# Gram products of a gated delta rule in four column tiles, with the order of the last stores and scalings changed

## The reference, cut to what matters

```
q = l2norm(silu(conv(x @ Wq))) * SCALE; k = l2norm(silu(conv(x @ Wk))); v = silu(conv(x @ Wv))
for t in range(512):
    S = S * exp(g[t])
    delta = (v[t] - k[t] @ S) * beta[t]
    S = S + outer(k[t], delta)
    o[t] = q[t] @ S
```

## Time and profile before

| | before |
|---|---|
| median of 3 runs | 2737.78 us (2733.69 to 2740.29) |
| profiled execution, its own time | 2728.86 us |
| its span | 2727.1 us |
| TensorE busy | 2487.7 us, 91% |
| VectorE busy | 1859.3 us, 68% |
| GpSimd busy | 1355.5 us, 50% |
| ScalarE busy | 1269.0 us, 47% |
| mean granted clock of TensorE | 0.955 |

### The profile page before, as it was taken

How to read it: one execution, slowest core, us unless ns; L and a number is a source line. 1 busy time by engine, 2 the same in 40 slices (tenths; PEclk the granted TensorE clock), 3 DMA queues, 4 the chain that set the end, 5 groups by cost and what they waited for, 6 DMA issues and landing times.

```text
span 2727.1 us, 33296 instructions
## 1 busy us (share of the span) xinstructions
PE 2487.7 (91%) x11786; PEld 1462.5 (54%) x11786; DVE 1859.3 (68%) x2240; ACT 1269.0 (47%) x2029; POOL 1355.5 (50%) x609
## 2 busy tenths in 40 slices
PE   7999949999999999999588899999989888999998
PEld 2554624444677999865133333333433333777776
DVE  5668875554655666676689889889988897722223
ACT  4434225531223666443557655765665442334333
POOL 0222338860050000250599999999999994222221
PEclk9989769989899999999799899999999999999999
DMA  6444874332063777641364674666567555000000
GB/s 229 143 124 105 96 117 97 89 101 93 12 232 134 266 271 269 205 133 41 112 197 160 178 225 164 205 193 194 180 202 213 185 206 210 1 1 16 16 0 31
DMA packets 246199, 384.98 MB, mean 141 GB/s; under 512 B 127104, under 2 KB 148608, under 8 KB 238624
## 3 DMA queue, kind: packets, MB, share of 16 engines
q1 hardware_dynamic: 232912, 335.45, 39.3%
q0 software_dynamic: 9296, 38.80, 5.7%
q10 hardware_dynamic: 3840, 8.72, 0.9%
HBM read 312.91 MB, written 59.51 MB: 137 GB/s over the span
## 4 chain that ended last, share of the span: by engine, by line
PE 58%; DVE 11%; POOL 9%; issue 8%; DMA 5%; SPq 4%; ACT 3%; POOLq 0%; ACTq 0%; DVEq 0%; PEldq 0%
PE psum L2058 7%; POOL arena L813 5%; PE psum L2005 4%; PE psum L2239 4%; PE psum L2240 4%; PE psum L2871 4%; POOL arena L805 3%; SPq L2317 3%; DMA arena<-bc_scr 3%; PE psum L3060 2%; PE psum L2212 2%; PE psum L2213 2%; PE psum L1901 2%; PE psum L485 2%; PE psum L1903 2%
## 5 line engine op out<-in xcount | busy, mean ns | idle before, releaser
L805 POOL TENSOR_TENSOR arena<-arena 128x2048 f32<-128x2048 f32 x128 | 600.8, 4694 | 110.0 <-DVE arena L1570 76.6
L2058 PE MATMUL psum<-arena,cst 128*128 128x512 f32 x1024 | 496.7, 620 | 93.9 <-POOL arena L813 84.1
L1106 ACT ACTIVATE psum<-arena,negA 128x512 f32<-128x512 f32 x512 | 333.6, 682 | 281.2 <-DVE arena L1585 240.5
L2058 PEld LDWEIGHTS psum<-arena,cst 128*128 128x128 f32 x1024 | 187.0, 193 | 385.8 <-issue 206.5
L1585 DVE TENSOR_TENSOR_SCAN arena<-psum,arena 128x512 f32<-128x512 f32 x256 | 310.8, 1214 | 99.5 <-POOL arena L805 57.8
L813 POOL TENSOR_TENSOR arena<-arena 128x1024 f32<-128x1024 f32 x128 | 324.0, 2531 | 18.2 <-DVE arena L1585 9.1
L1585 DVE TENSOR_TENSOR_SCAN psum<-psum,arena 128x512 f32<-128x512 f32 x256 | 296.8, 1204 | 0.0
L857 POOL TENSOR_TENSOR arena<-arena 128x512 f32<-128x512 f32 x64 | 92.4, 1443 | 325.5 <-ACT arena L1230 300.5
L2005 PE MATMUL psum<-arena 128*128 128x512 f32 x512 | 230.7, 594 | 1.3 <-PE psum L2005 0.8
L2403 POOL TENSOR_TENSOR arena<-arena,cst 128x512 f32<-128x512 f32 x64 | 76.2, 1218 | 257.4 <-DVE arena L2723 165.3
L2239 PE MATMUL psum<-r 128*128 128x512 f32 x512 | 202.8, 396 | 1.0 <-issue 1.0
(11 more groups left out here) (374 smaller groups left out, 5017.4 us busy)
## 6 DMA issues: line engine op xcount, KB each, us to landing
arena<-bc_scr SPq DMA_DIRECT2D x256, 512.0 KB, 4.8
arena<-w_exp SPq DMA_DIRECT2D x23, 1408.0 KB, 6.3
arena<-in_gu SPq DMA_DIRECT2D x48, 512.0 KB, 5.1
arena<-in_inw SPq DMA_DIRECT2D x32, 512.0 KB, 3.7
arena<-in_dn SPq DMA_DIRECT2D x31, 512.0 KB, 6.9
x_scr<-arena SPq DMA_DIRECT2D x19, 512.0 KB, 5.9
arena<-in_x SPq DMA_DIRECT2D x8, 1024.0 KB, 9.6
w_exp<-in_gu SPq DMA_DIRECT2D x16, 512.0 KB, 6.8
```

What stands on the lines that cost most here:

```text
L805: nc.gpsimd.tensor_tensor(dB[:, at:at + 2], du[:, j:j + 2].unsqueeze(1).broadcast_to([P, 2, 2, T]), BR[:, q % 2].unsqueeze(2).broadcast_to ...
L1106: nc.scalar.activation(psum[:, bank], dt[:, b % 2, j + t], ACT.Exp, scale=negA2[:, at:at + 1]).then_inc(s["da_ok"], 1)
L2058: ins = mm(psum[:, t], ident, dB[:, k % NSLOT, t], start=False, stop=(n == NS - 1), skip_group_check=True)
```

## The change

The Gram products swap their operands. The chunk's keys and queries, kept side by side in `KQC`, are now the weights, 128x32, and the block diagonal slot is moved through, 128 columns. Four chunks go to four column tiles, one PSUM bank takes a group of 16. The result is turned, so ScalarE copies it to SBUF (`gram_copy`) and TensorE transposes it in four pieces (`gram_turn`) into the bank that VectorE masks from. In passes 1 to 3 there is one bank for products and one for the transposed group; after the last pass two and two. Further:

- ScalarE writes the keys beside the queries (`keys_beside`) once a batch.
- `gram_evict` 0, 1 and 2 move behind `conv_tile` 3, 5 and 7.
- In pass 3 SP stores the Gram rows of batch 2 before it waits for the inverse of batch 1; the eight stores of that inverse go to ScalarE's queue.
- After the last pass ScalarE spreads the four slots of group 2 (eight instructions), GpSimd the rest; eviction 3 of batch 3 comes after row 12 of the inverse of batch 2 instead of after row 14; both halves of V are scaled after the last inverse.
- On SP's queue, the eight large loads of V for the second head group all come behind the stores of the inverse of batch 2, where four of them stood before, and four small ones of the first head group move behind the last Gram rows.

```diff
...
-KQ = view(0, 8192, "p (s l t) -> p s l t", s=2, l=TL)
+KQ = view(0, 4096, "p (s l t) -> p s l t", s=1, l=TL)
+KQC = view(4096, 4096, "p (u g c m) -> p u g c m", u=2, g=HG, c=NCH)
 QT = view(8192, 4096, "p (l t) -> p l t", l=TL)
...
     if b == B - 1:
-        at = qks[:, n % 4]
+        at = vst[:, n % 4] if n // 4 % 4 == 2 else qks[:, n % 4]
     else:
...
+def gram_tmp(b, k):
+    return MT[:, 4 * (k % 2)] if b == B - 1 else MT[:, 0] if b == B - 2 else LTB[:, B - 1]
+def gram_banks(b, k):
+    return (k % 2, 2 + k % 2) if b == B - 1 else (0, 1)
 def key_rows(b, i):
-    return acc[:, i] if b == B - 1 else KQ[:, 1, i * B + B - 1]
+    return acc[:, i] if b == B - 1 else MT[:, 4 * i + 1] if b == B - 2 else (LT, LTB)[i][:, TL - 1]
 dec = sb("dec", [P, 4, TL * NCH])
...
                 values(0, h, 0, B - 1, "v_in")
-        if b >= 2:
+        if b == B - 2:
             inverse_out(b - 2)
...
             gram_out(b - 1)
+        if b == B - 1:
+            sp.wait_ge(s["pt_ok"], b - 1)
+        if b:
             gram_in(b - 1)
...
+    keys_out(B - 1)
     sp.wait_ge(s["vt_out"], 16 * B)
-    for h in range(8):
-        values(0, h, B - 1, B, "v_in")
     for h in range(4):
-        values(1, h, 0, B, "v_in1")
-    keys_out(B - 1)
+        values(0, h, B - 1, B, "v_in")
     sp.wait_ge(s["g_out"], 16 * B)
...
     gram_in(B - 1)
-    inverse_out(B - 2)
     for h in range(4, 8):
+        values(0, h, B - 1, B, "v_in")
+    inverse_out(B - 2)
+    for h in range(8):
         values(1, h, 0, B, "v_in1")
...
         l, t = k // 8 * B + b, 64 * (k % 8)
+        if n >= 16 * (B - 1) + 8 and n < 16 * (B - 1) + 12:
+            continue
         if k == 0:
...
         if n >= 4:
-            pool.wait_ge(s["g1_mm"], n - 3)
+            pool.wait_ge(s["g1_mm"], n - 7 if n >= 16 * (B - 1) + 12 else n - 3)
         nc.gpsimd.tensor_tensor(gram_slot(b, n).rearrange("p c (h j) -> p c h j", h=8),
...
             act.wait_ge(s["k_out"], 32 * b)
+        if b == B - 2:
+            act.wait_ge(s["m_out"], 32)
         nc.scalar.copy(key_rows(b, i), psum[:, ring_bank("k", b, i)]).then_inc(s["kc_ok"], 1)
+    def gram_copy(b, k):
+        n = 4 * b + k
+        act.wait_ge(s["g1_mm"], 4 * n + 4)
+        act.wait_ge(s["g1_t"], n - 1 if b == B - 1 and k > 1 else 4 * b if b == B - 1 else n)
+        if b >= B - 2:
+            act.wait_ge(s["m_out"], 16)
+        nc.scalar.copy(gram_tmp(b, k), psum[:, gram_banks(b, k)[0]]).then_inc(s["gc_ok"], 1)
+    def keys_beside(b):
+        act.wait_ge(s["bc_used"], 4 + 4 * (b + 1))
+        nc.scalar.copy(KQC[:, b % 2, :, :, 0:CH],
+                       KQ[:, 0, b::B].rearrange("p g (c i) -> p g c i", i=CH)).then_inc(s["gc_ok"], 1)
     for b in range(B):
...
                                      scale=convw[:, c, 3:4]).then_inc(s["first_ok"], 1)
+                if b and c == 0:
+                    keys_beside(b - 1)
                 if b and c in (1, 3):
...
                                      ACT.Sqrt, bias=epsc[0:64, 0:1]).then_inc(s["std_ok"], 1)
+            if b and c in (1, 3, 5, 7):
+                gram_copy(b - 1, c // 2)
         for i in range(4):
...
         for i in range(4):
+            if b == B - 1 and i == 2:
+                act.wait_ge(s["pt_ok"], b - 1)
+                for h in range(8):
+                    act.dma_start(t_scr[b - 2, 16 * h:16 * h + 16].rearrange("j (l q r) -> q (j l) r", l=HG, q=16),
+                                  PT[b - 2][16 * h:16 * h + 16].rearrange("p j (l u) i -> p (j l) (u i)", u=2)
+                                  ).then_inc(s["t_out"], 16)
             act.wait_ge(s["g_mm"], 8 * b + 4 + i + 1)
...
     act.wait_ge(s["conv_ok"], 2 + NQKV * B)
+    keys_beside(B - 1)
     keys_copy(B - 1, 0)
     keys_copy(B - 1, 1)
+    l, t = 1 * B + B - 1, 0
+    for h in range(8):
+        ins = nc.scalar.activation(vst.rearrange("p j (c m) -> p (j c) m", c=4)[:, :, CH * h:CH * h + CH],
+                                   KQ[:, 0, l, 0:256].rearrange("p (c j) -> p c j", j=CH),
+                                   ACT.Identity, scale=bmask[:, h:h + 1])
+    ins.then_inc(s["ka_ok"], 1)
+    for k in (0, 1, 2, 3):
+        gram_copy(B - 1, k)
...
         n, l, at = 4 * b + k, k // 2 * B + b, slice(256 * (k % 2), 256 * (k % 2) + 256)
-        dve.wait_ge(s["g1_mm"], 4 * n + 4)
-        g = psum[:, n % 2].rearrange("p (c w i) -> p c w i", w=2, i=CH)
+        dve.wait_ge(s["g1_t"], n + 1)
+        g = psum[:, gram_banks(b, k)[1]].rearrange("p (c w i) -> p c w i", w=2, i=CH)
         v.tensor_tensor(MT[:, l, at].rearrange(c3, i=CH), g[:, :, 0], LTB[:, l, at].rearrange(c3, i=CH), ALU.mult)
...
                 dve.wait_ge(s["zr_out"], 16 * NZERO)
+            if b == 3 and hg == 1:
+                dve.wait_ge(s["k_out"], 64)
             dve.wait_ge(s["ab_mm"], 2 * b + hg + 1)
...
         decay_columns(0)
-        evict(0)
         conv_tile(3)
+        evict(0)
         invert(8, 10)
         conv_tile(4)
-        evict(1)
         invert(10, 11)
...
         conv_tile(5)
+        evict(1)
         invert(11, 12)
...
         conv_tile(6)
-        evict(2)
         invert(12, 13)
         conv_tile(7)
+        evict(2)
         dve.wait_ge(s["std_ok"], b + 1)
...
         invert(13, 16)
-        if b == B - 1:
-            dve.wait_ge(s["k_out"], 32 * b)
         for i in range(4):
             dve.wait_ge(s["bc_mm"], 4 * b + i + 1)
-            dst = KQ[:, 1 - i // 2, (i % 2) * B + b]
-            v.scalar_tensor_tensor(out=dst, in0=qks[:, i], scalar=SCALE if i < 2 else 1.0,
-                                   in1=psum[:, 3 - i % 2], op0=ALU.mult, op1=ALU.mult).then_inc(s["bc_used"], 1)
+            if i < 2:
+                v.scalar_tensor_tensor(out=KQC[:, b % 2, i, :, CH:2 * CH], in0=qks[:, i].rearrange(c3, i=CH), scalar=SCALE,
+                                       in1=psum[:, 3 - i % 2].rearrange(c3, i=CH), op0=ALU.mult, op1=ALU.mult).then_inc(s["bc_used"], 1)
+            else:
+                v.scalar_tensor_tensor(out=KQ[:, 0, (i % 2) * B + b], in0=qks[:, i], scalar=1.0,
+                                       in1=psum[:, 3 - i % 2], op0=ALU.mult, op1=ALU.mult).then_inc(s["bc_used"], 1)
         dve.wait_ge(s["bc_used"], 4 + 4 * (b + 1))
         for hg in range(HG):
-            ch.link(v.tensor_tensor(QT[:, hg * B + b], KQ[:, 1, hg * B + b], tmpA[:, 2 + hg], ALU.mult))
+            ch.link(v.tensor_tensor(QT[:, hg * B + b].rearrange(c3, i=CH), KQC[:, b % 2, hg, :, CH:2 * CH],
+                                    tmpA[:, 2 + hg].rearrange(c3, i=CH), ALU.mult))
     dve.wait_ge(s["ab_used"], 2 + 2 * B)
...
     inverse_first(B - 2)
-    for k, (i0, i1) in enumerate(((1, 8), (8, 10), (10, 13), (13, 15))):
+    for k, (i0, i1) in enumerate(((1, 8), (8, 10), (10, 12), (12, 13))):
         inverse_rows(B - 2, i0, i1)
         gram_evict(B - 1, k)
-    inverse_rows(B - 2, 15, 16)
-    dve.wait_ge(s["v_in"], 256)
-    ch.link(v.tensor_tensor(V[:, 0:B], V[:, 0:B], bcol[:, 0:B].unsqueeze(3).broadcast_to([P, B, NCH, DV]), ALU.mult))
+    inverse_rows(B - 2, 13, 16)
     inverse_first(B - 1)
     inverse_rows(B - 1, 1, CH)
+    dve.wait_ge(s["v_in"], 256)
+    ch.link(v.tensor_tensor(V[:, 0:B], V[:, 0:B], bcol[:, 0:B].unsqueeze(3).broadcast_to([P, B, NCH, DV]), ALU.mult))
     dve.wait_ge(s["v_in1"], 128)
...
-        n, l = 4 * b + k, k // 2 * B + b
-        if n >= 2:
-            pe.wait_ge(s["g_ev"], n - 1)
+        n = 4 * b + k
+        to = psum[:, gram_banks(b, k)[0]]
+        pe.wait_ge(s["gc_ok"], 5 * b + 1 + k - (b == B - 1 and k > 0))
         for j in range(4):
-            pe.wait_ge(s["kx_ok"], 4 * n + j + 1)
+            if b == B - 1 and k == 2:
+                pe.wait_ge(s["ka_ok"], 1)
+            else:
+                pe.wait_ge(s["kx_ok"], 4 * n + j + 1 - 4 * (b == B - 1 and k == 3))
             for c in range(4):
-                at, t = 32 * (4 * j + c), 256 * (k % 2) + CH * (4 * j + c)
-                ins = mm(psum[:, n % 2, at:at + 32], gram_slot(b, j)[:, c], KQ[:, :, l, t:t + CH], start=True, stop=True)
+                ins = mm(to[32 * c:32 * c + 32, colq[j]], KQC[:, b % 2, k // 2, 16 * (k % 2) + 4 * j + c], gram_slot(b, 4 * n + j)[:, c], start=True, stop=True)
             ins.then_inc(s["g1_mm"], 1)
+    def gram_turn(b, k):
+        n = 4 * b + k
+        pe.wait_ge(s["gc_ok"], 5 * b + 2 + k)
+        if n:
+            pe.wait_ge(s["g_ev"], n - (b == B - 1 and k > 0))
+        for t in colq:
+            ins = nc.tensor.transpose(psum[:, gram_banks(b, k)[1], t], gram_tmp(b, k)[:, t], ident)
+        ins.then_inc(s["g1_t"], 1)
     for b in range(B):
...
                 gram_group(b - 1, c // 2)
+            if b and c in (2, 4, 6):
+                gram_turn(b - 1, c // 2 - 1)
         for i in range(4):
             gate_tile(i)
+            if b and i == 0:
+                gram_turn(b - 1, 3)
         pe.wait_ge(s["rinv_ok"], b + 1)
...
     keys_t(B - 1, 1)
-    for k in range(4):
-        gram_group(B - 1, k)
```

(9 more changed lines are left out.)

20 lines of the change are left out of this document (10 added, 10 removed).

## The result

| | before | after |
|---|---|---|
| median (range, runs) | 2739.61 us (2733.69 to 2748.72, 5) | 2762.47 us (2755.95 to 2765.45, 5) |
| ratio, 95% interval | | 1.0074 (1.0054 to 1.0093) |
| profiled execution, its span | 2728.86, 2727.1 us | 2758.65, 2756.9 us |
| mean granted clock | 0.955 | 0.954 |
| TensorE, VectorE busy | 2487.7, 1859.3 us | 2451.3, 1867.5 us |

The change made the kernel 22.9 us slower in the medians. The forecast was 11.1 us: the direction was right, the size half, and 2762.47 lies above the forecast range of 2731 to 2755. TensorE has 36 us less to do and the program is longer, as in the forecast.

The account below looks back on a forecast made before the run. TensorE narrowly bounds pass 1, VectorE passes 2 and 3; behind them VectorE, DMA and SP's queue take turns. 5.4 + 1.0 + 0.3 + 4.4 = +11.1 us on the median 2737.78 gave 2748.9, range 2731 to 2755.

Parts of the forecast that it names:

- pass 1: Projection stage, batch 1: TensorE's waits for later evictions, with half clock behind them, delay the norms; +5.4 us.
- pass 2: Projection stage, batch 2: VectorE sets it and reaches the norms almost together with TensorE; +1.0 us.
- the end: Behind the stage: Gram rows leave 9.6 us sooner, SP's queue adds 2.0 + 12.0 before the inverse's stores; +4.4 us.
- VectorE's own durations: Projection stage: VectorE's scans, convolutions and evictions take the times read from the earlier trace, such as 11.75 us to eviction 0.
- Half clock: TensorE behind each new wait of the stage: runs at half clock for a while, adding 1.8 us.
- the wait for G: Behind the stage: VectorE's 5.56 us wait for batch 2's masked Gram rows shrinks to about 0.9, gain 4.7.
- Price of a group: Gram products on TensorE: four column tiles cut a group from 3.6 to 1.0 us, saving 26 us in twelve groups.
- The PSUM rule: Gram groups of the stage: tiling speeds the products, not the emptying of PSUM, which can become the limit; no size.
- (A): Rival, projection stage: the waits cost no half clock; +5.8 us, 2743.6; chance 0.15.
- (B): Rival, SP's queue: V issues at their mean cost; +6.7 us, 2744.5, chance 0.15; with (A) 2739, chance 0.07.
- (C): Rival, SP's queue: it keeps up and VectorE's inverse ends the stage, -9.6 there; 2735 or 2729.6; chance 0.16.
- (D): Rival, Gram groups: column tiles do not overlap, a group stays 3.5 us plus 0.4; 2760 and more; chance 0.05.

Follow-up runs that it names:

- experiment 2: The change with matmuls computing nothing wanted put into TensorE's two large waits of each pass; 2755.47 us, one run.
- experiment 1: The change with TensorE's transpositions of groups 1, 2 and 3 moved later, nothing else; median 2742.44 us, ratio 0.9988 to the kernel before.
- experiment 7: The change with transpositions of groups 1 to 3 later and four large V loads back ahead of the last Gram rows; 2722.00 us, ratio 0.9945.
- experiment 8: experiment 7 plus nine matmuls computing nothing wanted before the second norms of passes 2 and 3; median 2721.44 us, ratio 0.9928.
- experiment 5: The kernel before with only four large V loads moved behind the stores of the inverse of batch 2; 2746.47 us, one run.
- experiment 3: The change with VectorE's evictions 0 to 2 back at their places before it; 2756.45 us, one run.
- experiment 9: The kernel before with only the change's order behind the stage, Gram products and V loads untouched; median 2734.27 us, ratio 0.9985.
- experiment 4: The change with SP's eight V loads of pass 3 moved behind the store and loads of batch 2's Gram rows; 2764.52 us, one run.

## Why the forecast was right in direction and half in size

Of the 11.4 us that are missing in the forecast 2.9 lie in pass 1, 3.6 in pass 2, 2.1 in pass 3 and 2.8 in the end. Three steps failed. VectorE's own durations were taken as fixed, where they grow inside GpSimd's slots: the largest miss, in pass 2. Half clock was put at 1.8 us a wait, where it cost 2.3 to 2.4. And the wait for G was put at 0.9 us, where two waits of 5.5 stood. The chain of waits in which these terms stand was right. The upper end of the range, 2755, is also 3 us more than its own terms give (2737.8 + 10 + 4.4 = 2752).

**Price of a group, right.** 1.01 us for 1.0. TensorE's saving was real and, as forecast, not counted where it then waits.

**Pass 1, right in place, 2.9 us short.** Taken from the start of the pass (0.85 us later than before), VectorE's scans start at 97.6 (97.5 forecast); eviction 0 ends at 112.6 for 111.5, of which 0.9 is L2712 beside GpSimd's slots; scans 1 start at 120.2, 7.6 us later for 7.0, which is half clock at 2.4 for 1.8; eviction 1 ends 9.9 us behind that for 9.2, the scans L2704 at 2.12 where the row behind the earlier trace rows had 1.46; the norms start 23.6 behind it for 23.1, half clock again. So one term was mis-sized, half clock (1.8 from three waits of 2.6 us; waits of 5 to 6 cost 2.3 to 2.4, and experiment 2 measures 2.25), and one was missing, VectorE beside GpSimd. I had taken VectorE's durations from where they stood and not asked at what other time the slots would be spread once the groups moved; the earlier trace rows had 6.26 us between its scans and convolution 5, and the same work takes 4.7 in experiment 1 (116.39 to 121.07).

**Pass 2, VectorE last as forecast, +4.6 for +1.0.** VectorE's own list took 3.45 us more. In the forecast's terms: from the first scans to the end of eviction 0 it allowed 14.0 us and the trace has 16.0 (183.81 to 199.78), from the second scans to the norms 33.7 and the trace has 34.4 (206.86 to 241.28), and the first scans start 0.55 later than forecast, behind the slow row of 144. The step that failed is that VectorE's durations in the earlier trace rows would stay. That VectorE and TensorE would come to the norms almost together held: VectorE waits 0.64 us. Part of the difference is scatter: the list of the kernel before gave 81.60, 83.83 and 84.43 us in three kernels, that of the change 86.20, 86.12 and 86.12. Traces show what scatters: a wait of TensorE before the second norms. In experiments 1 and 7, which run the same list there, TensorE's timeline reads, in experiment 1:

```profile
225.85 3.78 PE L2970 MATMUL psum<-arena,cst 32*128 32x512 f32 x4 [1.77 <-DVE arena L2769]
229.56 4.94 PE L2944 MATMUL psum<-arena,wab 128*48 128x512 f32 x8
```

and in experiment 7:

```profile
225.03 1.98 PE L2972 MATMUL psum<-arena,cst 32*128 32x512 f32 x4 [0.37 <-DVE arena L2771]
226.94 3.63 PE L2946 MATMUL psum<-arena,wab 128*48 128x512 f32 x8
```

A wait of 1.77 us with half clock behind it, 3.78 + 4.94 us, against one of 0.37 and full clock, 1.98 + 3.63; both sets start 75.1 us into the pass, so the 3.1 us between the two passes (84.60 and 81.54) are half clock alone, and experiment 8, with this wait filled, has 81.64. In experiment 7 TensorE had been slow earlier, a projection of 6.59 us behind a wait of 3.99, where VectorE was last anyway, and came to the norms without a wait. Where the clock falls decides it. Against the mean of the three (83.3) the change costs pass 2 2.9 us; pass 3, 79.8 in the mean, 1.8. The forecast of 1.0 and 0.3 stays too small, since it left VectorE's slowing out. In pass 3 VectorE is busy for 68.55 us where it was for 66.97, and it waits 1.54 us for the second decay product (292.02), where it had waited 0.85 for the first.

**The end, +7.2 for +4.4.** Term by term: eviction 3 sooner by 4.9, right. G sooner by 4.7: not there, and the step that failed is the wait of "about 0.9", what the eight issues leave behind the norm products. It left out that SP's store stands behind projection 7 (the V loads wait for it) and 15 us of V issues, and that the stage's own waits push projection 7 back; experiment 1, where they don't, has 4.4 of it. From eviction 3 to the stores 43.6 us for 30.3, +13.3, where 2.0 + 12.0 were forecast, right (experiment 5 has 11.8 for the four large ones). From the stores to the chain 9.8 for 11.0, where no change was forecast: -1.2.

**The rules.** The PSUM rule cited in the forecast holds: with the products at 1.0 us TensorE waited 32.1 us in eight waits of the stage for evictions (L2659), and in experiment 3, where they came sooner, 22.0 for the copies out of PSUM. But it was their order and not their amount: in experiment 1 the same evictions, from later places of the transpositions, cost 6.1 us in three waits. A rule that bears on the missing term was not used: the Trainium skill (SBUF — State Buffer, Who interferes with whom) has VectorE and GpSimd share a pair of SBUF ports, and a VectorE instruction with two inputs in SBUF contend there with a GpSimd instruction that reads SBUF, while one with at most one such input, outside the modes of two ports, does not. The rows agree: L2712 and L2704, with both operands in SBUF, lose 0.9 us inside a slot, about the 1.05 us that one slot instruction takes alone (GpSimd's at 327.54 in experiment 9), and the convolutions, with one in PSUM, lose nothing. The small copies, with one input in SBUF, lose too (0.97 us for 0.19 at 194.18), and no run here shows which mode they ran in.

**Rivals.** (A), no half clock: refuted, pass 1 with it is 4.5 us longer than without. (B), issues at the mean: refuted, 19.28 and 19.41 us for eight. (C), the queue keeps up: refuted for this placing, SP is 13.2 us late. In experiment 7, with four loads moved ahead, it nearly does (1.7 us). (D), tiles that don't overlap: refuted at 1.01 us. That a faster outcome was there, with the same tiles, I did not see: I never asked whether another place for the turns would keep the gain.

**What stays open.** That GpSimd's slots slow VectorE rests on durations that coincide in time; no run took the slots away. Of the loss in pass 2, how much is the slots and how much their new place relative to the inverse's rows was not tried separately. The 6.5 us by which the rest of the span differs between the two profiled executions is not explained.

## What to carry to other kernels

When a product gets cheap by leaving its result turned, the work that turns it back is in a chain (copy, transposition, eviction) across three engines: place each step behind work that covers the one it waits for (here two projections did), and look at which wait stands ahead of the next load or store. The same change is 0.7% slower or 0.6% faster by the places of three of the four transpositions of a pass and of four loads. And a gain behind a stage is only as good as the instruction that releases it: recompute every later term with the delay that the earlier ones cause.

## What the runs showed of the hardware

- VectorE's work slows beside GpSimd's: a scan of 128x512 from 1.22 to 2.12 us, a product from 0.68 to 1.58, a copy of 32 numbers from 0.19 to 0.97, all with their operands in SBUF and inside the time in which GpSimd spread slots. The convolution at 103.15, which reads PSUM inside that time, kept its 2.32 us for three instructions, and the product at 207.58 (L2703), which also reads PSUM, inside the slots of 207.21 to 213.14, its 0.69.
- Half clock behind a wait: 1.8 us after 2.6 us of idle time, 2.3 to 2.4 after 5 to 6 (2.1 in the same places of experiment 4); one of 1.77 us before the norms cost 3.1. The length of the wait alone does not give the price: behind 3.99 us a projection took 5.40 us in experiment 1 (293.41) and 6.59 in experiment 7 (207.83), where it takes 3.6 to 3.7 at full clock. Filling the time with products kept the clock at 0.98 over the pass. And in the kernel before the clock fell with no wait ahead of it: two projections behind a Gram group took 10.02 us at 182.71, where they took 7.11 at 107.32.
- Eight issues of 256 KB in pieces of 128 bytes take 19.3 us (17.6 to 20.6 in five other runs with the same loads), each time with four small stores of ScalarE's queue in that time or close behind; with eight such stores they take 23.7. Small stores of another engine's queue landed 2.8 us later in experiment 4, where eight loads of V in 192 KB each were issued at the same time.
- The four Gram groups behind the stage took 27.35 us in their old form at half clock, and 13.0 us in four column tiles with two of their turns and the waits for GpSimd's slots (313.70 to 326.69 in experiment 7).
